# One stage of a graph network on one core: leaky step and logits a round later, index loads tied to the gathers

## The reference

```python
h = silu(_ln(edge_scalars @ rw1 + rb1, rg1, rbe1))
h = silu(_ln(h @ rw2 + rb2, rg2, rbe2))
w = h @ rw3 + roff
ms = src_s[edge_src] + dst_s[edge_dst]          # gathered rows
mv = src_v[edge_src] + dst_v[edge_dst]
# ds, dv: products of w, ms, mv and the edge's unit vector
ls, lv = _eq_lin(ds, dv, lin_ws, lin_bs, lin_wv)
alpha, vs, vv = ls[:, :64], ls[:, 64:], lv      # logits' input and values
a = einsum('ehk,hk->eh', _smooth_leaky(alpha), alpha_dot)
amax = segment_max(a, edge_dst)                 # softmax over the edges of a node
```

## Time and profile before

| | us |
|---|---|
| median of 3 runs | 9317.33 |
| lowest and highest | 9287.5 and 9322.78 |
| profiled execution | 9334.97 |
| its span in the trace | 9333.2 |

### The profile page before, as it was taken

One profiled execution on the slowest core, in us unless ns is written; L12 is line 12 of the kernel. 1 busy time (PEld: TensorE's weight loads), 2 busy tenths in 40 slices (PEclk: granted clock), 3 DMA queues, 4 the chain that ended last, 5 costly groups with the idle time before them and its releaser, 6 DMA issues. The chain is left out here.

```text
span 9333.2 us, 186439 instructions
## 1 busy us (share of the span) xinstructions
PE 6919.9 (74%) x43168; PEld 6115.7 (66%) x43168; DVE 6350.6 (68%) x22528; ACT 4143.0 (44%) x9706; POOL 5188.6 (56%) x4620
## 2 busy tenths in 40 slices
PE   3556888888544787778899866799855559999555
PEld 2444666666444777777788766688744448999554
DVE  4555777777554888888666577666566667777677
ACT  1223444454222344444444477544355554444344
POOL 3455777777454444444455488555455544444677
PEclk8776778888555899999999999899977779999665
DMA  6764333333687333333345477545444444444455
GB/s 109 133 135 103 76 76 77 77 77 76 130 163 147 85 90 91 91 93 90 102 124 124 122 210 214 151 124 125 110 140 140 139 136 114 119 119 116 139 160 154
DMA packets 1017785, 1119.53 MB, mean 120 GB/s; under 512 B 490662, under 2 KB 678918, under 8 KB 1017312
## 3 DMA queue, kind: packets, MB, share of 16 engines
q1 hardware_dynamic: 835312, 812.90, 32.5%
q0 software_dynamic: 182144, 303.59, 14.4%
HBM read 650.50 MB, written 465.65 MB: 120 GB/s over the span
## 5 line engine op out<-in xcount | busy, mean ns | idle before, releaser
L665 POOL DMA_INDIRECT agg<-seg_rows,edge_idx x1568 | 1545.3, 986 | 891.4 <-issue 621.3
L444 POOL DMA_INDIRECT erow<-e_rows,edge_idx x1176 | 1246.3, 1060 | 1238.4 <-issue 1139.1
L714 POOL TENSOR_TENSOR stats<-stats,power 128x8 f32<-128x8 f32 (+1 forms) x588 | 757.0, 1287 | 1208.7 <-DVE stats L1030 384.4
L393 PE MATMUL banks<-w_all,xt 128*128 128x128 f32 (+1 forms) x2352 | 552.5, 372 | 609.4 <-DVE y_more L941 192.2
L479 PEld LDWEIGHTS banks<-seg,mid 128*128 128x128 f32 x7840 | 931.2, 194 | 15.6
L479 PE MATMUL banks<-seg,mid 128*128 128x128 f32 x7840 | 932.2, 277 | 0.0
L393 PEld LDWEIGHTS banks<-w_all,xt 128*128 128x128 f32 x2352 | 432.7, 249 | 699.8 <-issue 683.9
L527 ACT ACTIVATE mid_t<-banks 128x512 f32<-128x512 f32 x980 | 585.4, 597 | 315.0 <-PE banks L479 313.6
L396 PE MATMUL banks<-w_all,xt 128*128 128x128 f32 x3528 | 645.9, 334 | 0.0
L396 PEld LDWEIGHTS banks<-w_all,xt 128*128 128x128 f32 x3528 | 609.3, 250 | 0.0
L491 PE MATMUL banks<-w_all,mid_t 128*128 128x161 f32 (+1 forms) x2352 | 583.5, 330 | 2.8 <-ACT res L532 2.8
(11 more groups left out here) (267 smaller groups left out, 19003.8 us busy)
## 6 DMA issues: line engine op xcount, KB each, us to landing
x_rows<-xo SPq DMA_DIRECT2D x294, 324.0 KB
xin<-x_rows SPq DMA_DIRECT2D x294, 324.0 KB
e_rows<-ets SPq DMA_DIRECT2D x294, 322.0 KB
dst_row<-in_dst_flat SPq DMA_DIRECT2D x294, 256.0 KB
xin<-in_x SPq DMA_DIRECT2D x196, 324.0 KB, 8.8
seg_rows<-res SPq DMA_DIRECT2D x196, 322.0 KB
seg_rows<-res SPq DMA_DIRECT2D x98, 384.0 KB
seg_rows<-res SPq DMA_DIRECT2D x98, 338.0 KB
```

The lines of the kernel that those rows point to most:

```text
L393: pe.matmul(flat[:, to + k * cols:to + (k + 1) * cols], of[:, k * P:(k + 1) * P], W(w_s), start=True, stop=True)
L444: pool.indirect_dma_start(erow[s.quad][:, t, 0:EROW], None, table, bass.IndirectOffsetOnAxis(idx[s.slot][:, t:t + 1], 0),).then_inc(rows_i ...
L665: pool.indirect_dma_start(agg[s.quad][:, t, 0:SUM_COLS[layer]], None, seg_rows[layer], bass.IndirectOffsetOnAxis(idx[s.slot][:, t:t + 1], ...
L714: pool.tensor_tensor(st[:, at + n:at + 2 * n], st[:, at:at + n], power[:, 0:n], ALU.pow) \
```

## The change

In the logits stage:

- DVE's leaky goes from delay 5 to 6, PE's and ACT's logits and DVE's running_max from 6 to 7. leaky then stands in its round behind the first weights half with values of the round before.
- load_indices waits for the landed rows of chunk s.g - 2 (rows_in and rows_b_in), where it waited for that chunk's message to be finished.
- load_penalties goes from 5 to 6, store_values from 6 to 7, store_tops from 7 to 9.
- lg, the maxima (top, in the place of fm) and the value rows (rows_v, in the place of gate_v) have four buffers and a store semaphore for each, where they had two. One memset sets top[3], from which the first scan starts.

```diff
--- before.py
+++ after.py
@@ -214,7 +214,6 @@
         aux = two("aux", [P, TILES, AGG])
         gate = two("gate", [P, TILES, 96])
         stats = four("stats", [P, 96])
-        gate_v = two("gate_v", [P, TILES, D])
         fm, bm = two("fm", [HEADS, CHUNK]), two("bm", [HEADS, CHUNK])
         psum = ctx.enter_context(nc.psum_tensor("banks", [P, 8, 512], F32))
 
@@ -254,7 +253,8 @@
         soft_in = [signal(f"soft_in_{k}", 64, 2) for k in range(4)]
         soft_values = [signal(f"soft_values_{k}", 16, 2) for k in range(4)]
         pre_quad = [signal(f"pre_quad_{k}", 16, 2) for k in range(4)]
-        values_in, values_out = slots("values_in", 16), slots("values_out", 16)
+        values_quad = [signal(f"values_quad_{k}", 16, 2) for k in range(4)]
+        tops_quad = [signal(f"tops_quad_{k}", 32, 2) for k in range(4)]
         xt_mm, xt_sb = signal("xt_mm"), signal("xt_sb")
         hid_mm, hid_sb = signal("hid_mm"), signal("hid_sb")
         e_mm, e_sb = signal("e_mm"), signal("e_sb")
@@ -272,7 +272,6 @@
         logit_mm, logit_sb = signal("logit_mm"), signal("logit_sb")
         h1_mm, h2_mm, v1_mm, v2_mm, r1_mm, r2_mm = (signal(n) for n in ("h1_mm", "h2_mm", "v1_mm", "v2_mm", "r1_mm", "r2_mm"))
         sq1_sb, sq2_sb, all1_sb, all2_sb = signal("sq1_sb"), signal("sq2_sb"), signal("all1_sb"), signal("all2_sb")
-        tops_out = slots("tops_out", 32)
         var1_step, var2_step, ln1_step, ln2_step = (signal("var1_step"), signal("var2_step"),
                                                     signal("ln1_step"), signal("ln2_step"))
         silu1_sb, silu2_sb = signal("silu1_sb"), signal("silu2_sb")
@@ -1125,7 +1124,9 @@
                 mid, mid_t = two("mid", [P, TILES, 97 + 3 * P], own=own), sb("mid_t", [P, 4, CHUNK], own=own)
                 alpha, alpha_th = two("alpha", [P, TILES, C0], own=own), two("alpha_th", [P, TILES, C0], own=own)
                 leaky_x, lg_rows = sb("leaky_x", [P, TILES, C0], own=own), two("lg_rows", [P, TILES * HEADS], own=own)
-                pen, lg = two("pen", [HEADS, CHUNK], own=own), two("lg", [HEADS, CHUNK], own=own)
+                pen = two("pen", [HEADS, CHUNK], own=own)
+                lg, top = ([sb(f"{n}_{k}", [HEADS, CHUNK], own=own) for k in range(4)] for n in ("lg", "top"))
+                rows_v = [sb(f"rows_v_{k}", [P, TILES, D], own=own) for k in range(4)]
                 VAR, SECOND = 2 * P, 2 * P
 
                 @block.sync
@@ -1146,9 +1147,10 @@
                                      .rearrange("(t p) c -> p t c", p=P)).then_inc(attr_in[s.slot].sem, 16)
 
                     def load_indices(s):
-                        precompute(sp, mid_step.after((s.g - 1) * steps))
+                        precompute(sp, rows_in[s.slot].after(s.half), rows_b_in[s.slot].after(s.half))
                         sp.wait_ge(ready.sem, 1)
-                        sp.wait_ge(mid_step.sem, mid_step.after((s.g - 1) * steps))
+                        sp.wait_ge(rows_in[s.slot].sem, rows_in[s.slot].after(s.half))
+                        sp.wait_ge(rows_b_in[s.slot].sem, rows_b_in[s.slot].after(s.half))
                         sp.dma_start(idx[s.slot][:], inp["edge_idx"][bass.ds(s.g, 1)].rearrange("o p t -> (o p) t")) \
                             .then_inc(idx_in[s.slot].sem, 16)
 
@@ -1164,22 +1166,22 @@
                         sp.wait_ge(ready.sem, 1)
                         sp.wait_ge(val_sb.sem, val_sb.after(2 * s.g + 2))
                         sp.dma_start(values_dram[bass.ds(s.g * CHUNK, CHUNK), :].rearrange("(t p) c -> p t c", p=P),
-                                     gate_v[s.slot][:]).then_inc(values_out[s.slot].sem, 16)
+                                     rows_v[s.quad][:]).then_inc(values_quad[s.quad].sem, 16)
 
                     def store_tops(s):
                         precompute(sp, fmax_sb.after(s.g + 1), logit_sb.after(s.g + 1))
                         sp.wait_ge(ready.sem, 1)
                         sp.wait_ge(fmax_sb.sem, fmax_sb.after(s.g + 1))
                         sp.wait_ge(logit_sb.sem, logit_sb.after(s.g + 1))
-                        for k, what in enumerate((lg, fm)):
-                            sp.dma_start(tops_dram[:, k, bass.ds(s.g * CHUNK, CHUNK)], what[s.slot][:]) \
-                                .then_inc(tops_out[s.slot].sem, 16)
-
-                    pipeline(sp, chunks, [(load_scalars, 0), (load_vectors, 1), (load_indices, 2), (load_penalties, 5),
-                                          (store_values, 6), (store_tops, 7)])
-                    for k in range(2):
-                        sp.wait_ge(values_out[k].sem, values_out[k].after(chunks // 2))
-                        sp.wait_ge(tops_out[k].sem, tops_out[k].after(chunks // 2))
+                        for k, what in enumerate((lg, top)):
+                            sp.dma_start(tops_dram[:, k, bass.ds(s.g * CHUNK, CHUNK)], what[s.quad][:]) \
+                                .then_inc(tops_quad[s.quad].sem, 16)
+
+                    pipeline(sp, chunks, [(load_scalars, 0), (load_vectors, 1), (load_indices, 2), (load_penalties, 6),
+                                          (store_values, 7), (store_tops, 9)])
+                    for k in range(4):
+                        sp.wait_ge(values_quad[k].sem, values_quad[k].after(of_quad[k]))
+                        sp.wait_ge(tops_quad[k].sem, tops_quad[k].after(of_quad[k]))
 
                 @block.gpsimd
                 def _(pool):
@@ -1304,7 +1306,7 @@
                         last.then_inc(logit_mm.sem, 1)
 
                     pipeline(pe, chunks, [
-                        (r2, 3), (r1, 1), (h1, 0), (h2, 2), (logits, 6), (messages_t, 5),
+                        (r2, 3), (r1, 1), (h1, 0), (h2, 2), (logits, 7), (messages_t, 5),
                         (lambda s: variance(s, sq_1, 4, sq1_sb, v1_mm), 0), (lambda s: variance(s, sq_2, 5, sq2_sb, v2_mm), 2),
                         (lambda s: values(s, 0), 5), (lambda s: weights(s, 0), 3),
                         (lambda s: values(s, 1), 5), (lambda s: weights(s, 1), 3)])
@@ -1342,21 +1344,21 @@
 
                     def values(s, r):
                         if r == 0:
-                            act.wait_ge(values_out[s.slot].sem, values_out[s.slot].after(s.half))
+                            act.wait_ge(values_quad[s.quad].sem, values_quad[s.quad].after(s.quarter))
                             act.wait_ge(leaky_step.sem, leaky_step.after((s.g - 1) * 3))
                         act.wait_ge(val_mm.sem, val_mm.after(2 * s.g + r + 1))
                         ps, two_ = psum[:, 3, 0:448].rearrange("p (t c) -> p t c", t=2), slice(2 * r, 2 * r + 2)
                         act.activation(alpha_th[s.slot][:, two_], ps[:, :, 0:64], ACT.Tanh, scale=0.5)
                         act.activation(alpha[s.slot][:, two_], ps[:, :, 0:64], ACT.Copy)
-                        act.activation(gate_v[s.slot][:, two_, 0:64], ps[:, :, 64:128], ACT.Copy)
-                        act.activation(gate_v[s.slot][:, two_, 64:].rearrange("p t (c i) -> p t i c", i=3),
+                        act.activation(rows_v[s.quad][:, two_, 0:64], ps[:, :, 64:128], ACT.Copy)
+                        act.activation(rows_v[s.quad][:, two_, 64:].rearrange("p t (c i) -> p t i c", i=3),
                                        ps[:, :, 128:].rearrange("p t (i c) -> p t i c", i=3), ACT.Copy) \
                             .then_inc(val_sb.sem, 1)
 
                     def logits(s):
                         act.wait_ge(logit_mm.sem, logit_mm.after(s.g + 1))
-                        act.wait_ge(tops_out[s.slot].sem, tops_out[s.slot].after(s.half))
-                        act.activation(lg[s.slot][:], bank(2, HEADS), ACT.Copy).then_inc(logit_sb.sem, 1)
+                        act.wait_ge(tops_quad[s.quad].sem, tops_quad[s.quad].after(s.quarter))
+                        act.activation(lg[s.quad][:], bank(2, HEADS), ACT.Copy).then_inc(logit_sb.sem, 1)
 
                     pipeline(act, chunks, [
                         (lambda s: roots_all(s, 48, all_2, r2_mm, all2_sb, s.g + 3), 3),
@@ -1365,7 +1367,7 @@
                         (lambda s: squares(s, 5, 1, h2_mm, h2_t, sq_2, sq2_sb, ln2_step, 2, v2_mm), 2),
                         (lambda s: silu(s, x_2, u_2, 4, ln2_step, 2, w_mm, 2, silu2_sb), 3),
                         (lambda s: silu(s, x_1, u_1, 2, ln1_step, 1, h2_mm, 1, silu1_sb), 1),
-                        (logits, 6), (messages_t, 5),
+                        (logits, 7), (messages_t, 5),
                         (lambda s: values(s, 0), 5), (lambda s: values(s, 1), 5)])
 
                 @block.vector
@@ -1454,16 +1456,17 @@
                         dve.wait_ge(logit_sb.sem, logit_sb.after(s.g + 1))
                         dve.wait_ge(fmax_sb.sem, fmax_sb.after(s.g))
                         dve.wait_ge(pre_in[s.slot].sem, pre_in[s.slot].after(s.half + 1))
-                        dve.wait_ge(tops_out[s.slot].sem, tops_out[s.slot].after(s.half))
```

(12 more changed lines are left out.)

## The result

The changed kernel took 9171.33 us (median of 4 runs, 9150.39 to 9187.61) against 9316.9 us (4 runs) of the kernel before on the same chip: ratio 0.9849, 95% interval 0.982 to 0.9878. The profiled execution took 9187.61 us.

What follows compares the result with a forecast made beforehand. The prediction took the logits stage as bound by a PE and ACT loop of 13.8 us, with POOL's floor of 14.0 us beside it. Terms -33 + 3 = -30 us took the median 9317 to 9287 us; range 9225 to 9335.

Steps and rivals of the forecast that it cites:

- The diff touches nothing else that runs: Opening step: only the logits stage, 1522 us of a span of 9333.2 us, was taken to be affected.
- The h1 waits, 33 us: PE's h1 product: earlier index load removes at most 42.1 us of waits for scal_e and issue; 33 us reach the round.
- The leaky move, worth 0 by itself beside a lead for POOL: DVE's tail: ln2 some 1.3 us earlier, covered by ACT, worth 0; POOL's lead of 0.6 to 1.3 us passes the gain.
- rounds shorter by a whole microsecond at the same granted clock: Sign of error in the logits stage's profile after: it would mean that DVE's tail was on the path.
- Sum for the stage, -30 us: Logits stage: 33 us gained at h1, 3 us taken off for POOL's limit, everything else 0; stage at about 1492 us.
- Rival 1, the clock: Logits stage: fewer PE gaps lift the mean clock by 0.05, 47 us more gain, 9240 us in all; chance 0.23.
- The 9.5 us per unit and round: Logits stage: cost of a round per unit of granted clock, from rounds of 13.8 us at 1.00 and 17.5 at 0.61.
- Rival 2, POOL's floor of 14.0 us: Logits stage: POOL's gathers and pow hold fast rounds at 14.0 us, so nothing is gained, 9317 us; chance 0.17.
- Rival 3, pow beside leaky: Logits stage: POOL's pow grows 0.86 us beside DVE's leaky, 42 to 60 us slower, 9359 to 9377 us; chance 0.06.
- The buffers, the memset, the drain: 0: Logits stage: four buffers, one added memset (0 to 1.3 us) and SP's two extra rounds (0 to 2 us), each taken 0.

Runs made afterwards that it cites:

- b_shift6_3: Kernel before with 12 already met waits (six instructions) in DVE's setup; on the third chip 9227.99 us, ratio 0.9865 (0.9857 and 0.9881 on the first two).
- the filler: Three matmuls per chunk with unread results, in PE's wait for the mid_t copies; added to the changed kernel: 9018.88 us, ratio 0.9726.
- a_node_fit: Changed kernel with 280 already met waits (140 instructions) in DVE's setup; ratio 0.9862.
- a_leaky_old_3: Changed kernel with leaky, logits and maxima in their old rounds and DVE's later loops kept in place; ratio 0.9906 on the third chip.
- idx_old_fill3: Changed kernel with three unread matmuls per chunk on PE and load_indices waiting for the message again; 8995.81 us, ratio 0.9705.
- a_fill3_2: Changed kernel with three unread matmuls per chunk on PE, both edits kept; 9004.46 us, ratio 0.9716.
- leaky_old_fill3: Changed kernel with three unread matmuls per chunk on PE and leaky, logits and maxima in their old rounds; 9000.49 us, ratio 0.9712.
- b_fill3: Kernel before with DVE's loops placed as in the changed kernel and three unread matmuls per chunk on PE; 9080.32 us, ratio 0.9795.

## Why the prediction was wrong, point by point

**"The diff touches nothing else that runs"** is the step that failed. It was true of the work and false of the code: 123 of the 146 us (b_shift6_3) come from six instructions by which a later loop of DVE was moved. The sum had no term for it, and by this the time fell below the range; what the logits stage gained, 35 us, lies inside it. Both signs were there beforehand: queue 14 on the page of before, and in the other stage's list of waits one for "issue" of up to 7.4 us, 22 times at one instruction.

**The h1 waits, 33 us.** That they go was right, and so was the size at a given clock: 33 us are 0.34 us for each of 98 rounds, and 0.3 to 0.5 us was measured. Wrong was that this reaches the stage. The index move by itself left the stage 9 us longer on the third chip, and its ratio lies 0.004 to 0.006 above b_shift6's on three chips; each pair of intervals overlaps, the sign was three times the same.

**The leaky move, worth 0 by itself beside a lead for POOL.** Mis-sized. The prediction said that rounds shorter by a whole microsecond at the same granted clock would prove it wrong, with DVE's tail on the path. They came: with both edits 14.03 to 12.86 us at full clock, 16.55 to 15.59 between 0.70 and 0.85, where the index move alone gives 0.3 to 0.5 us. Where the clock of the stage was low, the leaky move alone took 67 and 52 us out of it (1822 to 1755, 1895 to 1843), and both edits together 62 on the first chip (1760). Why it should do so there, where h1 hardly waits, isn't settled: the stage's mean clock was 0.02 higher with it. At the usual clock it was run alone only with the filler.

**Sum for the stage, -30 us.** Measured: 35, 29 and 37 us (1530, 1536 and, in a_node_fit, 1528 us against 1565, the last two on another chip than the 1565). The prediction took the stage for 1522 us, 840 to 2362; from its first to its last instruction it is 1565, which changes no term. By the times it is 146 - 123 = 23 us, less than their intervals. That the number was near is luck: at a like clock the edits give about twice as much, the clock takes most of that back in the middle rounds, and two thirds of what is left lie at the stage's ends.

**Rival 1, the clock.** The lever is real, and its sign for this change was not as I had it: the index move alone went with 0.77 for 0.81, both edits with 0.79 for 0.80. The 9.5 us per unit and round hold up: 0.81 of clock to 0.77 costs 98 x 9.5 x 0.04 = 37 us by it, about what the index move gained at h1 (the sorted rounds of before give 9.7 us per unit from 1.00 down to their mean of 0.74, but 13.5 down to 0.68). Without the filler the index move alone went with no higher clock of the stage on any of the three chips; work in the larger gap raised it (0.79 to 0.90: 98 x 9.5 x 0.11 = 102 us by the slope, 110 measured). With that gap filled, each edit went with a higher clock (0.89 to 0.93 and more), as the rival has it. The Trainium skill, "TensorE: Matmul & The Clock Gate", section "HAM oscillation — how this bites in real kernels", advises to keep PE from idling. The filler's result agrees, and so do the edits beside the filler; a_leaky_old_3, with one idle gap less and a lower clock (0.77 for 0.81), does not.

**Rival 2, POOL's floor of 14.0 us.** Not a floor at that height: 13.5 us without a wait. In after the full-clock rounds take 12.86 us, all eight of them behind a round in which POOL had waited 2.35 us for the message, so with a lead.

**Rival 3, pow beside leaky.** Hardly seen in after, though 78 of its 94 pows run beside a step of leaky: the median is 2.30 us as before, and one takes 2.50 us where none of before took over 2.32. With the filler it is seen where leaky stands a round later: 28 of 94 pows take over 2.34 us in idx_old_fill3, 20 in a_fill3_2, the longest 2.58, and none in leaky_old_fill3 and b_fill3. One of them:

```profile
875.39 0.42 DVE L1443 SCALAR_TENSOR_TENSOR leaky_x<-alpha_th,alpha 128x256 f32<-128x256 f32 x1
875.40 2.57 POOL L1201 TENSOR_TENSOR stats<-stats,power 128x12 f32<-128x12 f32 x1
875.84 0.43 DVE L1446 TENSOR_TENSOR leaky_x<-leaky_x,w_all 128x256 f32<-128x256 f32 x1
```

So beside leaky's steps pow is stretched in some rounds, by 0.28 us at most and not by the 0.86 us that the rival took; leaky's steps keep their 0.42 us. The 28 rounds add up to 5.5 us of pow over 2.30 us each.

**The buffers, the memset, the drain: 0.** No run speaks against it, and none took them apart.

## What to carry to other kernels

Before a gain or a loss is given to an edit, compare the stages that the edit doesn't touch: a loop whose waits for "issue" come once a turn, with packets on the instruction queue, won or lost 120 us here by six instructions ahead of it, and a few waits that are already met put it back. A wait taken from TensorE is earned only if the clock stays (here it fell by 0.04 without the filler and rose by 0.08 with it, both with the index move); read the length of rounds at a like clock and the mean clock apart. Where a gap of TensorE is left in each round, cheap matmuls in it can be worth more than the edit under study: 110 us here, against some 25 us for both edits.

## What the runs showed of the hardware that was not expected

- Instructions come in packets of 8 KB (286 packets, 2.34 MB; 128 instructions each, if one takes 64 bytes). A DVE loop of 268 was fetched anew in each turn or not at all, by its position, with a period of 128 or a part of it; if three blocks are what stays, 11 of 128 positions are bad ones (worked out: a start at 117 or later in its block reaches into a fourth). A loop of 423 was fetched anew in all kernels.
- The same logits stage was granted 0.79 on some chips and 0.65 to 0.70 on others, 1566 against 1822 and 1895 us for one and the same kernel. Ratios on one chip can be compared; times between chips can't.
- Fewer waits of TensorE can go with a lower clock (0.81 to 0.77 with the index move alone) or with a higher one (0.89 to 0.97 with the same edit beside the filler). Why is open. In a_leaky_old_3 PE's busy time rose, 1182.71 to 1212.47 us in 1400, as the lower clock makes its matmuls longer.
- A pow on POOL beside DVE's steps with two inputs took up to 2.58 us for 2.30, in 28 of 94 rounds at most, and in 64 overlaps in leaky_old_fill3 not once.
